# Two graph layers on one core: transposes in 64-row halves and one score tile per step of attention

## The reference

```python
h = relu(layernorm(x))                               # layer 1: 6 heads of 64
q, k, v = heads(h @ Wq + bq), heads(h @ Wk + bk), heads(h @ Wv + bv)
probs = softmax(q k^T / 8 + (0 where adj, else -9e15))
x = x + (probs v) @ Wf + bf
h = relu(layernorm(x))                               # layer 2: 12 heads of 32
f = einsum(h, W);  s, d = tanh(f) . w_src, tanh(f) . w_dst
attn = softmax(where(adj, leaky_relu(s_i + d_j), -999))
o = elu(attn f + b);  g = sigmoid(h @ H_w.T + H_b)
x = x + g * o + (1 - g) * h
```

## Time and profile before

| | us |
|---|---|
| median of 3 runs | 1798.54 (1797.27 to 1798.77) |
| time of the profiled run | 1799.47 |
| span of the profiled execution | 1797.7 |
| one graph in the steady state | 108.7 |
| mean granted clock of TensorE | 0.990 of 2.4 GHz |

### The profile page before, as it was taken

How to read it: one execution, slowest core, us unless ns; L and a number is a source line. 1 busy time by engine, 2 the same in 40 slices (tenths; PEclk the granted TensorE clock), 3 DMA queues, 4 the chain that set the end, 5 groups by cost and what they waited for, 6 DMA issues and landing times.

```text
span 1797.7 us, 39493 instructions
## 1 busy us (share of the span) xinstructions
PE 1674.6 (93%) x12528; PEld 1021.2 (57%) x12528; DVE 1335.1 (74%) x3130; ACT 1101.8 (61%) x2231; POOL 1033.7 (58%) x1287
## 2 busy tenths in 40 slices
PE   5899999999999999999999999999999999999885
PEld 4464655647465574645657465574655646556461
DVE  4778687786878768677786877768777786876847
ACT  2666566665666656566665666666566665666653
POOL 4356565674656656565564646646565565655735
PEclk9899999999999999999999999999999999999998
DMA  4000101001010010100001010010100101000000
GB/s 155 19 19 12 49 6 35 18 14 44 6 51 7 13 39 6 53 6 21 32 10 48 6 35 23 9 44 6 53 6 13 39 9 50 6 18 19 10 10 18
DMA packets 38114, 46.46 MB, mean 26 GB/s; under 512 B 2624, under 2 KB 38080, under 8 KB 38080
## 3 DMA queue, kind: packets, MB, share of 16 engines
q1 hardware_dynamic: 38080, 46.03, 8.0%
HBM read 33.44 MB, written 12.58 MB: 26 GB/s over the span
## 4 chain that ended last, share of the span: by engine, by line
PE 72%; ACT 12%; DVE 8%; issue 6%; POOL 1%; DVEq 1%; DMA 0%; ACTq 0%; POOLq 0%
PE work L1099 16%; PE score L1099 16%; ACT arena L576 8%; PE acc L1258 8%; PE acc L1252 6%; PE acc L1190 5%; PE score L1156 4%; DVE arena L867 4%; PE work L1173 3%; PE work L1252 3%; PE score L1233 2%; PE acc L1211 2%; ACT arena L582 2%; PE score L1219 1%; PE work L1271 1%
## 5 line engine op out<-in xcount | busy, mean ns | idle before, releaser
L867 DVE SCALAR_TENSOR_TENSOR arena<-score,uqT,adjT 128x512 f32<-128x512 f32 x576 | 389.1, 744 | 35.7 <-PE score L1233 25.4
L416 POOL TENSOR_SCALAR arena<-arena,rinv 128x512 f32<-128x512 f32 x384 | 280.4, 746 | 185.8 <-DVE rinv L828 185.8
L576 ACT ACTIVATE arena<-sm,nmax 128x512 f32<-128x512 f32 x384 | 273.1, 713 | 128.8 <-DVE nmax L822 126.8
L450 POOL TENSOR_TENSOR arena<-arena,adjT 128x512 f32<-128x512 f32 x192 | 224.0, 1167 | 126.0 <-ACT arena L617 121.7
L822 DVE CUSTOM_DVE_ANT_0 sm<-score,mask 128x512 f32<-128x512 f32 x384 | 247.7, 685 | 60.4 <-PE score L1156 57.9
L1173 PEld LDWEIGHTS work<-ident_f,arena 64*128 64x128 f32 x3072 | 115.2, 140 | 185.9 <-issue 185.9
L1258 PE MATMUL acc<-arena,u_den 128*3 128x512 f32 x1536 | 200.8, 592 | 0.0
L1190 PE MATMUL acc<-arena,v_tok 128*64 128x512 f32 x768 | 198.7, 617 | 0.0
L423 POOL TENSOR_TENSOR rstd<-var,mhalf 128x1 f32<-128x1 f32 x128 | 68.7, 549 | 225.6 <-DVE var L786 225.6
L1173 PE MATMUL work<-ident_f,arena 64*128 64x64 f32 x3072 | 138.0, 229 | 60.5 <-ACT arena L582 40.9
L614 ACT ACTIVATE arena<-score,nqT 128x512 f32<-128x512 f32 x192 | 130.0, 677 | 103.3 <-PE score L1233 75.8
(11 more groups left out here) (168 smaller groups left out, 3952.2 us busy)
## 6 DMA issues: line engine op xcount, KB each, us to landing
x_in<-in_x SPq DMA_DIRECT2D x16, 768.0 KB, 4.6
xb<-in_x SPq DMA_DIRECT2D x16, 768.0 KB, 4.5
out_x<-xres SPq DMA_DIRECT2D x64, 192.0 KB, 1.9
adj_u<-in_adj SPq DMA_DIRECT2D x16, 256.0 KB, 2.8
arena<-in_wk SPq DMA_DIRECT2D x1, 576.0 KB, 6.1
arena<-in_wq SPq DMA_DIRECT2D x1, 576.0 KB, 7.2
arena<-in_wv SPq DMA_DIRECT2D x1, 576.0 KB, 8.5
arena<-in_wf SPq DMA_DIRECT2D x1, 576.0 KB, 9.5
```

The lines of the kernel that those rows point to most:

```text
L416: nc.gpsimd.tensor_scalar(pr, pr, rinv[:, p, t, i:i + 1], 1.0, ALU.mult, ALU.mult).then_inc(probs_ready, 1)
L450: nc.gpsimd.tensor_tensor(edge_at(n, HG - 1), t_ring[:, n % 2], adjT[:, n % TT], ALU.mult).then_inc(last_edge_ready, 1)
L576: nc.scalar.activation(probs[p % 2 * 2 + i][:, t], sm[:, n % NSM], ACT.Exp, scale=-1.0, bias=nmax[:, p, t, i:i + 1], accum_out=rsum[:, p, ...
L867: nc.vector.scalar_tensor_tensor(out=edge_at(n, j), in0=score[j][:], scalar=uqT[:, c, q:q + 1], in1=adjT[:, c], op0=ALU.max, op1=ALU.mult) ...
```

## The change

- The transposes of layer 2 (`norm2`, `tok`, `fin`) are made of pairs of 64-row halves into two banks at once, by `turn_halves`, for two row tiles together. Their copies (`turned_high2`, `turned_low2`, the `h_tok` copies, `inverse_den`, `divide`) read one half of two tiles each, and every one waits for the pair. The heads of a group are renumbered by `head_of`, so that half a bank holds whole heads.
- Attention has one score tile in each of seven steps, where two came after some steps and none after others. ACT, DVE and POOL have new orders.
- The next graph's normed tiles go one per step into acc1 (tiles 0 and 1) and acc0 (2 and 3), counted as banks 6 and 7. So PE waits for the low half of tile 0 ahead of tile 1, for `ctx_low(0)` ahead of tile 2, for the low half of tile 2 ahead of tile 3, and at the first context step of pairs 1 and 2 for the tile that was there.
- `values(b+1, 0)` goes ahead of the aggregation, `values(b+1, 1)` to where 0 was; banks of `v` and `fin` alternate; tiles of `turn_sums` go in two pairs, the second behind `values(b+1, 3)`. `TANH_AT` moves three gate activations by a step or more.

```diff
+def head_of(g, j):
+    return j // 2 * 2 * NG + 2 * g + j % 2
...
-    ("v", 0): 1, ("v", 1): 1, ("v", 2): 1, ("v", 3): 0,
+    ("v", 0): 0, ("v", 1): 1, ("v", 2): 0, ("v", 3): 1,
...
-    ("num", 1): 0, ("fin", 0): 0, ("fin", 1): 0, ("fin", 2): 1, ("fin", 3): 1,
-    ("norm1", 0): 2, ("norm1", 1): 3, ("norm1", 2): 4, ("norm1", 3): 5,
+    ("num", 1): 0, ("fin", 0): 0, ("fin", 1): 1, ("fin", 2): 0, ("fin", 3): 1,
+    ("norm1", 0): 6, ("norm1", 1): 6, ("norm1", 2): 7, ("norm1", 3): 7,
...
-S_AFTER = {(0, 0): ((1, 1), (1, 2)), (0, 1): ((1, 3),), (0, 3): ((2, 0), (2, 1)), (1, 0): ((2, 2),), (1, 1): ((2, 3),)}
-NORM_AFTER = {(0, 2): (0, 1), (1, 2): (2, 3)}
...
+S_AFTER = {(0, 0): (1, 1), (0, 1): (1, 2), (0, 2): (1, 3), (0, 3): (2, 0), (1, 0): (2, 1), (1, 1): (2, 2), (1, 2): (2, 3)}
+NORM_AFTER = {(0, 1): 0, (0, 2): 1, (1, 1): 2, (1, 2): 3}
...
-             ("gate", 0), ("gate", 1), ("uq", 0), ("gate", 2), ("gate", 3), ("q", 2), ("num", 1), ("v", 0)]
-          + both("s", 0, 0) + both("s", 0, 1) + [("v", 1), ("fin", 0)] + both("s", 0, 2) + [("v", 2), ("fin", 1)]
-          + both("s", 0, 3) + [("fin", 2), ("v", 3), ("fin", 3)] + both("s", 1, 0))
+             ("gate", 0), ("gate", 1), ("uq", 0), ("gate", 2), ("gate", 3), ("v", 0), ("q", 2), ("num", 1), ("v", 1)]
+          + both("s", 0, 0) + both("s", 0, 1) + [("fin", 0), ("fin", 1)] + both("s", 0, 2) + [("v", 2)]
+          + both("s", 0, 3) + [("v", 3), ("fin", 2), ("fin", 3)] + both("s", 1, 0))
...
-                drained(pool, b, "tok", c)
+                drained(pool, b, "tok", c // 2 * 2)
+                drained(pool, b, "tok", c // 2 * 2 + 1)
...
             def attention(g, fin):
-                for t in range(TT):
+                for t in range(3):
                     normalise(g, 1, t)
                 if fin:
                     add_out(g - 1, 0)
+                normalise(g, 1, 3)
                 normalise(g, 2, 0)
                 if fin:
                     add_out(g - 1, 1)
...
             def attention(g, more, fin):
                 pT_copy(g, 0, 0)
                 exps(g, 1, 1)
+                pT_copy(g, 0, 1)
                 exps(g, 1, 2)
-                pT_copy(g, 0, 1)
+                if more:
+                    turned_high1(g + 1, 0)
+                pT_copy(g, 0, 2)
                 exps(g, 1, 3)
+                if more:
+                    turned_high1(g + 1, 1)
                 if fin:
                     elu(g - 1, 0)
-                pT_copy(g, 0, 2)
-                if more:
-                    turned_high(g + 1, 0, 0)
-                    turned_high(g + 1, 0, 1)
                 pT_copy(g, 0, 3)
                 exps(g, 2, 0)
+                pT_copy(g, 1, 0)
+                ctx_high(g, 0)
+                exps(g, 2, 1)
                 if fin:
                     elu(g - 1, 1)
-                exps(g, 2, 1)
-                pT_copy(g, 1, 0)
-                ctx_high(g, 0)
+                pT_copy(g, 1, 1)
+                if more:
+                    turned_high1(g + 1, 2)
                 exps(g, 2, 2)
-                pT_copy(g, 1, 1)
+                pT_copy(g, 1, 2)
+                if more:
+                    turned_high1(g + 1, 3)
                 exps(g, 2, 3)
                 if fin:
                     elu(g - 1, 2)
-                pT_copy(g, 1, 2)
-                if more:
-                    turned_high(g + 1, 0, 2)
-                    turned_high(g + 1, 0, 3)
                 pT_copy(g, 1, 3)
+                if more:
+                    ctx_high(g, 1)
+                    qk_hi_copy(g + 1, 0, "k")
+                pT_copy(g, 2, 0)
+                if not more:
+                    ctx_high(g, 1)
                 if fin:
                     elu(g - 1, 3)
...
                 for n in range(STEPS):
                     last_maxima(b, n)
-                    if n < 3:
-                        tanh_gate(b, n + 1)
+                    if more and n == 1:
+                        value(b + 1, 0)
+                    if n in TANH_AT:
+                        tanh_gate(b, TANH_AT[n])
                     if more and n == 4:
                         qk_hi_copy(b + 1, 2, "q")
                     if n % TT == 1 and n > 1:
                         sums_copy(b, n // TT - 1)
                     if more and n == 8:
-                        value(b + 1, 0)
+                        value(b + 1, 1)
                 if more:
                     exps(b + 1, 0, 0)
                 sums_copy(b, NG - 1)
                 if more:
-                    value(b + 1, 1)
                     exps(b + 1, 0, 1)
                     value(b + 1, 2)
                     exps(b + 1, 0, 2)
...
             def attention(g, more, fin):
                 pT_copy(g, 0, 0)
+                inverse(g, 1, 0)
                 maxima(g, 1, 1)
+                pT_copy(g, 0, 1)
                 maxima(g, 1, 2)
-                inverse(g, 1, 0)
-                pT_copy(g, 0, 1)
                 inverse(g, 1, 1)
-                maxima(g, 1, 3)
                 if fin:
                     dve.wait_ge(gate_ready, g * TT)
                     dve.wait_ge(h2p_ready, g * TT)
                     positive(g - 1, 0)
                 pT_copy(g, 0, 2)
+                if more:
+                    turned_low1(g + 1, 0)
+                maxima(g, 1, 3)
                 inverse(g, 1, 2)
                 if fin:
                     difference(g - 1, 0)
+                pT_copy(g, 0, 3)
+                if more:
+                    turned_low1(g + 1, 1)
                 inverse(g, 1, 3)
-                if more:
-                    turned_low(g + 1, 0, 0)
-                    turned_low(g + 1, 0, 1)
-                pT_copy(g, 0, 3)
                 maxima(g, 2, 0)
                 if fin:
                     positive(g - 1, 1)
+                pT_copy(g, 1, 0)
+                ctx_low(g, 0)
+                inverse(g, 2, 0)
                 maxima(g, 2, 1)
-                pT_copy(g, 1, 0)
-                inverse(g, 2, 0)
                 if fin:
                     difference(g - 1, 1)
+                pT_copy(g, 1, 1)
                 maxima(g, 2, 2)
                 inverse(g, 2, 1)
-                pT_copy(g, 1, 1)
-                ctx_low(g, 0)
-                maxima(g, 2, 3)
-                inverse(g, 2, 2)
+                if more:
+                    turned_low1(g + 1, 2)
                 if fin:
                     positive(g - 1, 2)
                 pT_copy(g, 1, 2)
+                maxima(g, 2, 3)
+                inverse(g, 2, 2)
+                if more:
+                    turned_low1(g + 1, 3)
+                pT_copy(g, 1, 3)
                 inverse(g, 2, 3)
                 if fin:
                     difference(g - 1, 2)
-                if more:
-                    turned_low(g + 1, 0, 2)
-                pT_copy(g, 1, 3)
-                if more:
-                    turned_low(g + 1, 0, 3)
+                    positive(g - 1, 3)
+                if more:
+                    ctx_low(g, 1)
+                    qk_low(g + 1, 0, "k")
+                pT_copy(g, 2, 0)
+                if not more:
...
                 if fin:
...
+                    difference(g - 1, 3)
                 pT_copy(g, 2, 1)
...
@@ -1031,14 +1086,22 @@
                     maxima(b + 1, 0, 0)
                 dve.wait_ge(agg_done, (b + 1) * STEPS)
                 nc.vector.tensor_copy(denT, acc[1][:]).then_inc(den_drained, 1)
-                for t in range(TT):
-                    if more and t < TT - 1:
-                        maxima(b + 1, 0, t + 1)
-                    if more:
-                        inverse(b + 1, 0, t)
-                    inverse_den(b, t)
-                    divide(b, t)
-                if more:
+                if more:
+                    maxima(b + 1, 0, 1)
+                    inverse(b + 1, 0, 0)
+                for m in range(2):
+                    inverse_den(b, m)
+                    divide(b, m)
+                if more:
+                    maxima(b + 1, 0, 2)
+                    inverse(b + 1, 0, 1)
+                    maxima(b + 1, 0, 3)
+                    inverse(b + 1, 0, 2)
+                for m in range(2, 4):
+                    inverse_den(b, m)
+                    divide(b, m)
+                if more:
+                    inverse(b + 1, 0, 3)
                     maxima(b + 1, 1, 0)
...
+            def turn_halves(banks, blocks, source):
+                for t in range(2):
+                    for c in range(blocks):
+                        for half in range(2):
+                            rows = slice(half * DH0, (half + 1) * DH0)
+                            at = (t * blocks + c) * DH0
+                            ins = nc.tensor.transpose(banks[half][0][:, at:at + DH0], source(t, c)[rows],
+                                                      ident_f[rows, rows])
+                            if (t, c) == (1, blocks - 1):
```

(46 more changed lines are left out.)

191 lines of the change are left out of this document (102 added, 89 removed).

## The result

The changed kernel takes 1933.68 us (median of four runs, 1929.07 to 1937.01) against 1797.9 for the kernel before on the same chip: a ratio of 1.0753, with a 95% interval of 1.0729 to 1.0777. It is slower by 135.8 us, half again the 91 forecast, and inside the range by 1.3 us. The profiled run took 1934.79 us.

A forecast was written before the change was run, and what follows sets the result against it. PE sets third pair, front and steps; DVE nearly fills attention's first two pairs; a chain over engines sets the tail. 74 (attention), 13.5 (tails), 1, 3 and -0.8 make +91 on 1798.54: 1889, range 1815 to 1935.

The forecast's parts named there:

- The walk: Attention's first two pairs, step by step: interlocking orders on DVE, ACT and POOL end them at 28.2, before 22.89: +5.3 us.
- Rival C: As forecast, and PE's clock also falls after the tail in each graph: +2.5 us, 15 times, 1926; chance 0.09.
- Tail: From `scores(b+1,0,1)`: `turn_probs(0,0)` starts at 12.79 against 11.89, +0.9 us, although PE has 2.6 us less to do.
- lower bound of -1.5: The tail's best case: only POOL's 0.35 + 1.36 behind the earliest inverse, at 9.2.
- Adds 0.46: Aggregation steps: `values(b+1,0)` ahead of step 0 adds 1.70 - 1.24 = 0.46 us, offset by 0.42; steps end unchanged.
- part 1: Half-height transposes in layer 2: token tiles save about 0.5 us of PE, transposed query rows stand 0.42 earlier.
- `norm2` saves nothing: Layer 2's normed tiles in halves: no gain, since each pair must wait for its later tile, where PE stands anyway.
- Copies: Strided copies of 384 elements from the half transposes: no change, bounds -0.1 and +0.2 us each for twelve.
- A: Waits interlock less and PE's shorter work decides: attention 21.6 us or -1.3, time taken at 1770; chance 0.12.
- B: Gains of the tail and losses of attention cancel: within 4 us of 1798.5; chance 0.05.
- Last graph: The last graph, which has no norm tiles: 3 us more.
- keeps its 13.65: Attention's third pair with its key products: PE has its own work again, so its 13.65 us stay.

The follow-up runs named there:

- c1_fill: The changed kernel with twelve products more, never read, ahead of `turn_probs(0,0)` where PE waits: 1949.56 us, ratio 1.0841.
- p2_attention: The kernel before with the change's attention and nothing else of it: 1893.22 us, ratio 1.0531.
- b3_tail: The kernel before with `values(b+1,0)` ahead of the aggregation and the tail reordered, sums still turned one full tile at a time: 1781.94 us, ratio 0.9909.
- b4_tok: As b3_tail, with the token tiles (`turn_feat`) in pairs of halves too: 1775.2 us, ratio 0.9871 against the kernel before.
- b1_pad84: The kernel before with 84 more semaphore increments of PE a graph, seven at each of twelve places: 1812.14 us, ratio 1.0078.
- b1_pad36: The kernel before with 36 more semaphore increments of PE a graph, three at each of twelve places: profiled run 1799.75 us.
- a1_elu: The changed kernel with ACT's `elu(0)`, `elu(1)` and `elu(2)` moved ahead of the exponentials of their step: 1917.45 us, ratio 1.0655.
- a3_both: The changed kernel with `elu` ahead of the exponentials on ACT and `normalise(1,3)` ahead of `add_out(0)` on POOL: 1902.68 us, ratio 1.0581.

## Why the prediction was right or wrong

**Attention: right in mechanism and order, 0.9 us short in size.** The walk had `turn_probs` at 1.6, 4.59, 8.35, 14.4, 15.98, 21.1 and 24.26 and the key product at 28.2. The trace has them at 1.75, 5.66, 9.30, 15.18, 16.83, 21.96, 25.21 and 29.1, counted from 992.08. The difference is there by the third turn and then stays near 0.9. DVE stands 1.69 and 1.39 us at the two `difference` (walk: 1.84 and 1.5), and `normalise(1,3)` ends at 15.0 (walk: 14.25). The 0.9 is the clock, which c1_fill takes away: there the turns stand at 1.65, 4.59, 8.43, 14.30, 15.95, 21.08 and 24.34 and the key product at 28.21, each within 0.1 of the walk. So 14 times 5.33, 74.6 us, is what the forecast had as 74, and 12.9 more are the clock. The size still depends on how the tail hands over: in p2_attention, behind the old tail, the first of these turns stands at 2.44 and attention takes 28.76 at a clock of 1.00.

**Rival C was true as well, at a price that I had too high.** The score group at 992.57 takes 0.66 us where those from 998.26 on take 0.49, and over that stretch the granted clock averages 0.63, so that it is at its lower level, 1.2 GHz, for some 3.4 us:

```profile
992.08:996.73 4.65, 4.65 (x48) 3.42 (x48) 2.86 (x8) 2.73 (x8) 1.36 (x2) 0.63 0.00 0
```

It fell right behind PE's wait of 2.60 us; in the steps before that tail PE was busy 32.40 of 32.40 us. I had kept it apart from the forecast with 0.09, for want of a gap as long in the trace before. That gap was in my own walk (2.9 us), and then the fall belonged in the sum. The Trainium skill, "TensorE: Matmul & The Clock Gate", HAM oscillation, describes waits that cost TensorE its clock each time round; the trace agrees, with a shorter wait than those of that section. It costs 0.9 us a graph here, not the 2.5 of the rival, and nothing in the graphs of p2_attention in which the fall comes 15.5 us or more into attention. The measured time is nearer to the 1926 of this rival than to the forecast, but by luck: the clock makes 12.9 us of the difference, the stall below 24.5.

**Tail: right, +0.7 against +0.9.** Second pair of sums at 8.54 (walk: 8.60), `turn_probs(0,0)` at 12.60 (12.79), and the named wait, for ACT's value copy, is there. b3_tail shows what the walk did not ask: with full tiles, and `inverse(0,3)` ahead of the last two divides, it takes 10.26. The pairs and the order round them come to 2.3 us: the second pair must write bank 1 and therefore stands behind `values` 3 and its copy, and `inverse(0,3)` stands behind its divides. Which of the two a better order would have saved was not tried. The change as a whole lost 0.7 in the tail because one part lost more than another won. (The lower bound of -1.5 does not follow from its terms: 9.2 + 0.35 + 1.36 is 10.9, or -1.0.) I had credited the pairs with -0.9 on PE, an engine that waits there.

**Front and steps: the offset failed.** "Adds 0.46, which eats the 0.42 of part 1" was to give 0, and the steps rose by 0.4 while the fronts (those without a long third pair ahead) fell by less than 0.1. The 0.46 is nearly right (32.40 and 32.44 against 32.01, with PE busy throughout). The 0.42 came, as 0.37, only where the normed tiles of layer 2 stay whole: 27.89 in b4_tok, 28.2 to 28.3 after. So "`norm2` saves nothing" should have been "`norm2` costs 0.3 to 0.4", by this comparison, for `norm2` was not tried alone: PE now waits for the second normed tile, and again at the `uq` rows, waits that neither the kernel before nor b4_tok has.

```profile
926.68 0.24 PE L1179 MATMUL score<-ident_f,hn 64*128 64x64 f32 x1 [0.49 <-DVE xres L894]
...
945.04 0.41 PE L1412 MATMUL score<-ident_f,uq_rows 44*128 44x44 f32 x4 [0.25 <-ACT uq_rows L746]
```

The token tiles took 1.29 us from their start to that of the product behind them (983.30 to 984.59), and take 0.89 in halves (940.47 to 941.36): 0.40 less where I had 0.5.

**Copies: right.** The mean duration of a `divide` is 557 ns before and after, of a copy to `h_tok` 497 and 496, of an `inverse_den` 228 and 223; the high halves of layer 2 take 497, where those of both layers took 486. So none of them changed by more than 0.01 us, inside the bounds of -0.1 and +0.2.

**Rivals A and B fell** with attention at 28 to 29 us: `elu(0)` was done later than DVE's maxima, not earlier. (A's 21.6 us do not come out of its terms either: eight steps of 2.3, with 0.4 more in four of them, are 20.0.)

**Last graph: 3 forecast, 8.1 measured.** With the attention alone it is 6.0 (31.97 to 37.94). I walked only graphs that have norm tiles. The other 2.1 are the clock: with the filler of c1_fill the same stretch takes 37.54, 2.5 less. First the changed kernel, then c1_fill:

```profile
1814.30:1854.39 40.09, 30.91 (x282) 16.12 (x282) 24.02 (x59) 20.95 (x49) 20.10 (x24) 0.83 0.06 21
```

```profile
1832.33:1869.87 37.54, 27.40 (x282) 13.60 (x282) 23.93 (x59) 20.80 (x49) 20.11 (x24) 0.95 0.06 22
```

**The third pair: "keeps its 13.65" held for its work and missed a stall behind it.** That is the step that failed outright, worth 24.5 us of 135.8 with the four long fronts behind it. With it the time left the forecast's 1889 far behind and stayed in the range by 1.3 us, which is luck: the range was made for errors of the walk, and has no term for a stall. The change has 40 more matmuls a graph (640 of 16 graphs by the busy lines), each with its weight load, and I costed them by their time on the engine alone. b1_pad84 shows the stall without any other part of the change, b1_pad36 (but for one pass) and b4_tok its absence with 36 and 27 more instructions, p2_attention its absence with the whole of the new attention. Four of the seven stalls of the changed kernel have a front of 29.6 to 29.7 behind them: the clock over it is 0.94 there and 1.00 in the front at 918.77, so the clock sometimes falls behind this gap too.

The Trainium skill, "Runtime: NRT & Kernel Launch", Instruction fetch mechanics, says that an engine's instructions come from a small store that is filled ahead in order, with room for 2048 instructions for PE, and that a taken branch makes the engine wait for a fetch when its target is not in the current window, which the page puts at two pages of 256. By the two pages the kernel before should stall too, with 1566 matmuls and weight loads a graph (twice 12528 by 16); it does not, and of the page's two figures the larger one is nearer. Counted in the traces from one jump back to the next, with its semaphore and register instructions, PE has 1744 instructions before, 1770 in b4_tok and 1780 in b1_pad36, without a stall that repeats, and 1828 in b1_pad84 and 1830 after, with it. The runs put the limit between 1780 and 1828 of these. An estimate from the page's figures, 2048 less one block of 256 that is being filled, is 1792; no run here shows that this is how it comes about. Packets of 16.4 KB (1.36 MB by 83) agree with the page's blocks of 256 instructions. None of this stood in the prediction.

**What stays open.** Why the stall is 0.9 us in one kernel and 2.65 in another, and why it comes at seven of 13 jumps back in the changed kernel and at all in a1_elu and a3_both, with the same number of instructions. The count separates the kernels that have it from those that do not; it says neither how large it is nor how often it comes.
